# A graph layer kernel: x copied to the scratch table inside DRAM, and the SRC order's scatters moved from the node pass to the dense pass

## The reference

```python
h = x @ Wn.T + bn ; e = edge_attr @ We.T + be
a = leaky_relu(sum((h[src] + e) * attn, -1), 0.01)
a = softmax of a over the edges of one dst
z = x + relu(segment_sum(h[src] * a, dst, N))
x1 = layernorm(z)
mean = segment_sum(x1[dst], src, N) / max(count(src), 1)
out = layernorm(x1 + x1 @ W1.T + b1 + mean @ W2.T + b2)
```

## Time and profile before

| | before |
|---|---|
| median of 3 runs (lowest, highest) | 1667.97 us (1666.65, 1668.83) |
| the profiled execution's own time | 1660.1 us |
| its span | 1658.3 us |
| PE, PEld | 76%, 64% of the span |
| DVE, ACT, POOL | 66%, 47%, 45% |
| DMA, HBM read and written | 188 GB/s, 182.2 MB and 130.0 MB |
| granted TensorE clock, mean | 0.901 |

### The profile page before, as it was taken

One profiled execution on the slowest core, in us unless ns is written; L12 is line 12 of the kernel. 1 busy time (PEld: TensorE's weight loads), 2 busy tenths in 40 slices (PEclk: granted clock), 3 DMA queues, 4 the chain that ended last, 5 costly groups with the idle time before them and its releaser, 6 DMA issues.

```text
span 1658.3 us, 26818 instructions
## 1 busy us (share of the span) xinstructions
PE 1265.2 (76%) x7210; PEld 1068.7 (64%) x7210; DVE 1094.4 (66%) x3970; ACT 782.0 (47%) x1768; POOL 750.0 (45%) x731
## 2 busy tenths in 40 slices
PE   4277865776000799985099999999999899999994
PEld 3166754665000688764088888888888688877784
DVE  8565585666322655441088888888888888777762
ACT  6243475442000344332067777777777455444442
POOL 1035652035555678788642013333332256555553
PEclk9688798998555899999599999999999999999997
DMA  8977588767999555554557678888887323232221
GB/s 286 300 185 214 172 261 268 234 228 236 335 343 344 141 83 83 82 70 51 95 179 223 218 237 265 263 269 267 262 271 254 128 80 98 87 95 88 90 81 46
DMA packets 134006, 311.40 MB, mean 188 GB/s; under 512 B 24605, under 2 KB 57972, under 8 KB 133928
## 3 DMA queue, kind: packets, MB, share of 16 engines
q1 hardware_dynamic: 91870, 245.02, 44.7%
q0 software_dynamic: 40128, 64.45, 18.2%
q10 hardware_dynamic: 1930, 1.06, 0.2%
HBM read 182.23 MB, written 129.96 MB: 188 GB/s over the span
## 4 chain that ended last, share of the span: by engine, by line
PE 44%; DMA 27%; POOL 12%; issue 8%; DVE 4%; ACT 2%; SPq 2%; POOLq 0%; ACTq 0%
PE bank L1250 25%; DMA aggn<-low_digits_scratch 7%; DMA X<-in_x,idx_src 7%; PE bank L1240 6%; DMA z_scratch<-yout 5%; POOL z_scratch L513 4%; DMA xin<-z_scratch,idx_src 4%; POOL out_rows L467 4%; POOL xin L464 3%; PE bank L1247 3%; PE bank L1228 3%; DMA z_scratch<-xin,idx_out 3%; PE bank L1295 2%; PE bank L1291 2%; PE bank L1179 1%
## 5 line engine op out<-in xcount | busy, mean ns | idle before, releaser
L1250 PE MATMUL bank<-w1T,xT 128*128 128x256 f32 x1968 | 490.7, 380 | 0.0
L1250 PEld LDWEIGHTS bank<-w1T,xT 128*128 128x128 f32 x1968 | 343.3, 190 | 66.3
L473 POOL DMA_INDIRECT order_scratch<-pay,rank_i x200 | 196.8, 984 | 230.6 <-DVE rank_i L846 95.9
L568 ACT ACTIVATE yout<-bank,nmr,rstd 128x256 f32<-128x256 f32 x492 | 251.2, 576 | 8.0 <-DVE nmr L754 8.0
L919 DVE BATCH_NORM_STATS2 stats<-xin 128x6 f32<-128x512 f32 x246 | 158.7, 686 | 111.3 <-DMA xin<-z_scratch 57.6
L559 ACT COPY xT<-bank 128x512 f32<-128x512 f32 x346 | 203.0, 588 | 36.3 <-PE bank L1240 25.0
L464 POOL DMA_INDIRECT X<-z_scratch,idx_dst x100 | 94.9, 949 | 257.1 <-DVE xin L751 191.1
L919 DVE BATCH_NORM_STATS2 stats<-bank 128x6 f32<-128x512 f32 x246 | 168.5, 694 | 59.9 <-PE bank L1250 59.5
L667 ACT COPY agg<-bank 128x257 f32<-128x257 f32 (+1 forms) x200 | 74.2, 371 | 219.3 <-PE bank L1295 212.5
L513 POOL DMA_INDIRECT z_scratch<-xin,idx_out x100 | 158.2, 1582 | 40.7 <-issue 26.9
L1179 PE MATMUL bank<-X 128*128 128x196 bf16 x800 | 100.1, 261 | 99.0 <-ACT sel L654 72.8
(11 more groups left out here) (187 smaller groups left out, 1911.7 us busy)
## 6 DMA issues: line engine op xcount, KB each, us to landing
yout<-in_x SPq DMA_DIRECT2D x97, 512.0 KB, 6.1
z_scratch<-yout SPq DMA_DIRECT2D x97, 512.0 KB, 7.1
xin<-z_scratch SPq DMA_DIRECT2D x97, 512.0 KB, 5.2
out_rows<-yout SPq DMA_DIRECT2D x97, 512.0 KB, 3.4
kB<-keys_scratch SPq DMA_DIRECT2D x50, 256.0 KB, 5.1
kB<-sorted_scratch SPq DMA_DIRECT2D x50, 256.0 KB, 3.4
aggn<-low_digits_scratch SPq DMA_DIRECT2D x50, 128.0 KB, 7.1
xin<-in_edge_attr SPq DMA_DIRECT2D x12, 512.0 KB, 7.1
```

The costliest lines, as they stand in the source:

```text
L473: g.indirect_dma_start(out=order_dram[k], out_offset=bass.IndirectOffsetOnAxis(ap=rank_i[k][:, t:t + 1], axis=0), in_=pay[:, t, :], in_off ...
L568: a.activation(yout[hu][0:rows, j, :], bank_of(j // 2)[0:rows, (j % 2) * D:(j % 2 + 1) * D], ACT.Identity, bias=nmr[0:rows, slot, j:j + 1] ...
L1250: ins = mm(to, buf[:, jj, c, 0:n], w[:, c, :], start=False, stop=i == len(terms) - 1 and c == 1)
```

## The change

The copy of x no longer passes SBUF. It is cut in `NCOPY` = 100 DMAs from DRAM to DRAM. Piece c takes, from each stretch of 400 nodes, the four nodes 4c to 4c + 3: 125 rows of 4 KB, 400 KB apart, 500 KB in all. SP waits for no landing of them; POOL waits once for all before the first add. The 100 pieces stand: 8 before the fifth block of edge features, one after the loads of each of the 25 DST groups, 24 after the loads of SRC group 1 (two at a time, each pair waiting for the one-hot digits of two more groups), 11 after the loads of the odd SRC groups 3 to 23, and 32 after the SRC sort. The DST order is read at SRC group 5 and no longer 12, ScalarE's store of the sorted keys moving with it (`ORDER_AT`). `FLIGHT` is 6 and no longer 4. The two SRC order scatters after each group of the node pass are gone; 80 instead of 30 of them lie in the dense pass, two in each of its first 40 groups, and the order is read at group 48 and no longer 24 (`HOOK`), so that the 100 gathers of neighbours' rows lie between groups 56 and 92 and no longer between 32 and 92. Four instead of two of these gathers may be open.

```diff
--- before.py
+++ after.py
@@ -21,11 +21,9 @@
 BF16 = mybir.dt.bfloat16
 I32 = mybir.dt.int32
 DST, SRC = 0, 1
-ORDER_AT = 12
-FLIGHT = 4
-COPY_FIRST = 12
-COPY_ONEHOTS = 14
-HOOK = 24
+ORDER_AT = 5
+FLIGHT = 6
+HOOK = 48
 
 
 def wait(eng, sem, value):
@@ -68,6 +66,8 @@
     assert 2 * HC <= 512 and LO == 2 * P and T % 4 == 0
     EC = 2 * GT
     NEC = FT // EC
+    NCOPY = 100
+    assert N % (NCOPY * GT) == 0
 
     z_dram = nc.dram_tensor("z_scratch", [N + 6 * P, D], F32).ap()
     keyrow_dram = [nc.dram_tensor(f"keys_scratch{k}", [T, P], F32).ap() for k in (DST, SRC)]
@@ -229,8 +229,7 @@
         s_sortd = sem("sorted_keys_in_dram")
         s_xones = sem("ones_columns")
         s_xg = sems("src_rows_gathered", FLIGHT)
-        s_cin = sems("copy_loaded", 4)
-        s_cout = sems("copy_stored", 4)
+        s_copy = sem("x_copied")
         s_zero = sem("spare_rows_cleared")
 
         s_xin = sems("x_loaded", 4)
@@ -280,7 +279,7 @@
         s_enm = sem("edge_r_scales")
         s_ey = sem("edge_y_ready")
         s_xs = sems("own_z_rows_gathered", 4)
-        s_nb = sems("neighbour_z_rows_gathered", 2)
+        s_nb = sems("neighbour_z_rows_gathered", 4)
         s_zsc = sems("z_rows_added", 4)
         s_ysc = sems("y_scattered", 4)
         s_rc = sems("reciprocals", 6)
@@ -334,27 +333,22 @@
                 sp.dma_start(xin[t][:, 0:2, :], w.rearrange("(b p) k -> p b k", b=2)).then_inc(s_w, 16)
             sp.dma_start(weT, We.rearrange("(b p) k -> p b k", b=2)).then_inc(s_w, 16)
 
-            copied = [0]
-
-            def copy(n):
-
-                for c in range(copied[0], min(copied[0] + n, G + 2)):
-                    if c < G:
-                        wait(sp, s_cout[c % 4], 16 * (c // 4))
-                        sp.dma_start(full(yout[c % 4])[0:parts(c)], grp(x, c, parts(c))).then_inc(s_cin[c % 4], 16)
-                    if c >= 2:
-                        h = c - 2
-                        sp.wait_ge(s_cin[h % 4], 16 * (h // 4 + 1))
-                        sp.dma_start(grp(z_dram, h, parts(h)), full(yout[h % 4])[0:parts(h)]).then_inc(s_cout[h % 4], 16)
-                copied[0] = min(copied[0] + n, G + 2)
-
-            copy(4)
             sp.wait_ge(s_wt, 3)
             sp.wait_ge(s_vu, 1)
 
+            copied = [0]
+
+            def part_of(table):
+                return table.rearrange("(r c k) d -> c r (k d)", c=NCOPY, k=GT)
+
+            def copy_x(n):
+                for c in range(copied[0], min(copied[0] + n, NCOPY)):
+                    sp.dma_start(part_of(z_dram[0:N])[c], part_of(x)[c]).then_inc(s_copy, 16)
+                copied[0] = min(copied[0] + n, NCOPY)
+
             for c in range(NEC):
                 if c == 4:
-                    copy(COPY_FIRST)
+                    copy_x(8)
                 wait(sp, s_eau, EC * (c - 3))
                 v = edge_attr[0:NEC * EC * P].rearrange("(c t p) d -> p c t d", p=P, t=EC)
                 sp.dma_start(full(xin[c % 4]).rearrange("p (t d) -> p t d", d=DE),
@@ -376,10 +370,12 @@
                     sp.dma_start(lowB[n % 2], spread(lowrow_dram[k], q)).then_inc(s_lb[n % 2], 16)
                     wait(sp, s_kbu, n - 1)
                     sp.dma_start(full(kB[n % 2]), spread(keyrow_dram[k], q)).then_inc(s_kb[n % 2], 16)
-                    if k == SRC and q == 0:
-                        copy(COPY_ONEHOTS)
-                    elif q % 3:
-                        copy(1)
+                    if k == DST or q >= 2 and q % 2:
+                        copy_x(1)
+                    if k == SRC and q == 1:
+                        for i in range(Q // 2):
+                            sp.wait_ge(s_onehot, Q + 2 * i + 1)
+                            copy_x(2)
 
             def load3(k, q):
                 if k == DST and q < 2:
@@ -392,7 +388,7 @@
             sp.wait_ge(s_sortd, 16)
             for q in range(2):
                 load3(DST, q)
-            copy(G + 2)
+            copy_x(NCOPY)
             for q in range(2, Q):
                 load3(DST, q)
 
@@ -501,8 +497,7 @@
                 sent[0] = min(sent[0] + n, T)
 
             order_src(20)
-            for u in range(4):
-                pool.wait_ge(s_cout[u], 16 * len(range(u, G, 4)))
+            pool.wait_ge(s_copy, 16 * NCOPY)
             pool.wait_ge(s_zero, 48)
 
             for q in range(Q):
@@ -512,7 +507,6 @@
                 for j in range(GT):
                     g.indirect_dma_start(out=z_dram, out_offset=column(idx_out[DST], GT * q + j), in_=xin[q % 4][:, j, :],
                                          in_offset=None, compute_op=ALU.add).then_inc(s_zsc[q % 4], 16)
-                order_src(2)
 
             for h in range((T - sent[0]) // 2):
                 pool.wait_ge(s_x1, GT * h + GT)
@@ -523,8 +517,8 @@
             pool.wait_ge(s_agg[DST], T)
             for t in range(T):
                 pool.wait_ge(s_x1, GT * (HOOK + 8 + (G - HOOK - 14) * t // T))
-                wait(pool, s_nb[t % 2], 16 * (t // 2))
-                gather(X[:, t, 0:D], z_dram, column(idx_dst[SRC], t), s_nb[t % 2])
+                wait(pool, s_nb[t % 4], 16 * (t // 4))
+                gather(X[:, t, 0:D], z_dram, column(idx_dst[SRC], t), s_nb[t % 4])
 
             for q in range(Q + 3):
                 if q < Q:
@@ -1036,8 +1030,8 @@
                 ins.then_inc(s_nst, 1)
 
             def first_neighbours():
-                for par in range(2):
-                    dve.wait_ge(s_nb[par], 16 * len(range(par, T, 2)))
+                for i in range(4):
+                    dve.wait_ge(s_nb[i], 16 * len(range(i, T, 4)))
                 for q in range(2):
                     neighbour_stats(q, q)
```

## The result

The changed kernel takes 1707.6 us (median of 4 runs, 1705.7 to 1711.7), the kernel before 1667.6: the ratio is 1.024, 95% interval 1.022 to 1.026. It is slower by 40 us; 1715 were forecast. The profiled execution took 1711.7 us, its span 1709.9, against 1660.1 and 1658.3: in the two traces there are 51.6 us to find.

The account below looks back on a forecast made before the run. Transfers, then POOL, were taken to bound the kernel; 1660.1 profiled, +55 for the first add behind the five-engine copy's end, -8 in the node pass give 1707, +8 for the median 1715. Range 1655 to 2000 (1668 to 1765: chance 0.52).

Parts of the forecast that it names:

- price of a 4 KB row: Time of one copied row on one DMA engine: 188 ns from mixed traffic, with 154 and 308 as ends.
- fifth edge block landed: Fifth block of edge features, behind eight copy pieces: lands at 66 where before 69.5, -4 us (-10; +20).
- DST sort: 25 sort groups, each with one piece behind its loads: 5.9 us a group for 5.7, +5 us (0; +78).
- long stretch: 24 pieces after SRC group 1's loads: 113 us where before 14 blocks took 51, +62 us (+41; +134).
- rest of the SRC sort: SRC groups after the 24 pieces: one group less, -4 us; groups falling towards 4.2 to 5.0 us, -15.
- tail: sort's end to first add: Last 32 pieces after the SRC sort: 150 us, plus 15 for gathers sharing the engines and 3 to land.
- node pass: Node groups without the two scatters: 10.0 us for 10.4, -8 us in all, not the scatters' 63.
- dense and source pass: Dense pass takes 50 more scatters and denser gathers beside a busy TensorE: 0 us taken, 10 allowed.
- median against the profiled run: Median of the runs lies 8 us above the profiled execution: 1707 becomes 1715.
- "The earlier order is worth nothing under the tail": DST order read 7 groups earlier starts gathers 39 us sooner, worth nothing unless the copy ends before 534.
- a row that counts twice (308 ns): Rival on the copy: a row inside DRAM pays for read and write, 1990 us; chance 0.22.
- that second rival: Rival on the copy: 125-row pieces fill all 16 engines, first add at 450, 1546 us; chance 0.12.

Follow-up runs that it names:

- the old copy without scatters: Kernel before, copy through SBUF, with only the new order places, more gathers in flight and no scatters in the node pass: 1645.4 us, ratio 0.988.
- the pair of kernels without that wait: The 16-engine copy with two spare-row sets, POOL waiting for the group before last: 1633.2 us on chip B; the same with scatters back: 1693.7.
- the 16-engine copy: Changed kernel with 98 pieces, each one block of 512 nodes as 128 adjacent 4 KB rows: 1548.8 us, ratio 0.930 on chip A.

## Why the prediction was right, point by point

The forecast came out at 1715 for 1707.6, and by the mechanism that it named first: **five engines carry the copy, and its tail sets the first add.** The signs named for it were there: a DMA share of 0.34 in the tail, POOL's wait ended by the copy, first add at 606 for 619, a wait for `aggn` of 60 us at SRC group 2 for some 50. Ten engines in place of five took 158 us away.

But the sum was nearer than its terms, and that was luck: a price too high, a term of the wrong sign and an allowance of the wrong sign made up for each other. Each against the trace after, in shifts against before:

| step | forecast (154 ns) | measured |
|---|---|---|
| price of a 4 KB row | 188 ns (154) | 153 to 156 ns |
| fifth edge block landed | -4 (-10) | 62.0 for 69.5: -7.5 |
| DST sort | +5 (0) | 73.00 to 220.14 for 80.34 to 222.64: +4.8 |
| long stretch | +62 (+41) | 220.14 to 312.65 for 222.64 to 273.47: +41.7 |
| rest of the SRC sort | -19 (-19) | 312.65 to 466.17 for 273.47 to 406.81: +20.2 |
| tail: sort's end to first add | 168 (141) | 139.9 |
| first add | +55 (-4) | +42.1 |
| node pass | -8 | 606.0 to 868.3 for 564.0 to 822.1: +4.1 |
| dense and source pass | 0 | 843.4 for 838.0: +5.4 |
| median against the profiled run | +8 | -4.1 |

- **The price was mis-sized.** I took the mixed window's 188 ns because a copy inside DRAM reads and writes; five engines ran at the price of the best slice. With 154 ns my sum was 1656, 51 us too low.
- **The rest of the SRC sort was wrong in sign**, 39 us off, and this made up for it. I let the groups fall to 4.2 to 5.0 us because the engines' load was under 5 us. But a group waits for its load's landing, not for a mean load: behind a piece a load is 3.9 us later on five engines, and VectorE and ScalarE stood: from 331 to 466 they waited 27 and 47 us for `aggn`, with ten engines, over the same groups, 4 and 18. `aggn` took 8.6 us in the median against 7.1. The load behind the long stretch added 8 us by itself, 17.1 for 8.8, since SyncE had its queue full. The runs with ten and sixteen engines have their SRC groups at 4.6 us with the pieces in the same places.
- **The node pass gave nothing.** That the scatters lay inside the wait for the landing was right, and it is shown by the old copy without scatters, whose groups kept their distance, and by the pair of kernels without that wait. The last 0.35 us a group that I still expected were not there (10.34 for 10.4). And the keys of group 2 behind the 32 pieces, which I named without a price, cost 5 us.
- **"The earlier order is worth nothing under the tail"** was 11 us off in the changed kernel: fewer gathers share the tail.
- **The dense pass** held, with gathers from group 56 to 92: the kernel with the old copy and the new places needs 834.6 us from its first dense load to its span's end, the kernel before 836.2. Of the 5.4 us of the changed kernel's trace, 4.6 lie in the source pass, which the change does not touch; its own runs differ by 6 us. Their cause was not tried.

- **The last 8 us** took the median to lie above the profiled execution, as before; this time it lay 4 us below.

Of the rivals, a row that counts twice (308 ns) is excluded by 153 to 156 ns, all sixteen engines by the 34%. What that second rival would give, 1546, is what a copy on sixteen engines then took, 1548.8: the sum was sound there, only the condition was not met.

## What to carry to other kernels

Before a DMA is reshaped, look at the count of its outermost rows: here 125 rows of 4 KB went over 5 of the 16 engines, 100 over 10, 128 over 16, and the first alone turned a gain of 7% into a loss of 2.4%. A queue shared by bulk pieces and small loads that are waited for prices the piece twice, once in the tail and once in every load behind it. And an instruction that lies inside a wait costs nothing and its removal gives nothing: the wait (here for a landing, by way of reused spare rows) is what to take away, and that gave 2.1 us a group.

## What the hardware showed that I had not expected

- A 4 KB row copied from DRAM to DRAM costs a DMA engine 153 to 156 ns when five engines work, no more than a load (154 ns in the best slice of before). With all sixteen it is 195 ns, with the gathers beside and in packets of 16 KB.
- The Trainium skill, "DMA: Bandwidth & Descriptors", section "Latency and other measured facts", has a full rate of 214 GB/s for copies between HBM tensors, from which I had estimated 306 ns. Here the copy moved 8.59 MB in 30 us, 286 GB/s, with the gathers beside it, and with ten engines and rows 500 KB apart 8.82 MB in 35 us, 252 GB/s. The measurement decides.
- SyncE's queue takes only so much ahead, and by these runs it is not pieces that count. On five engines issuing 24 took 85 us, and a load issued then landed 17.1 us later: some four pieces of 25 rows an engine, about 110 rows. On ten engines the load behind the last piece landed 14.5 us later: some nine pieces of 10 rows an engine, about 90 rows. The 30 last pieces on sixteen engines, in packets of 16 KB, were all issued in 19.9 us, long before they were carried. The row counts are estimates from these times.
- Ten engines were as good as sixteen: beside their pieces a gather took 5.4 us to land in the median, while beside contiguous 512 KB pieces on sixteen it took 15.9 us from 350 to 380. In the kernel before, with sixteen engines as full, it took 6.4 us; what delays it, the packets of 16 KB or the many pieces queued ahead, stays open.
- The kernel before took 1666, 1731 and 1721 us on three chips. With the same program, the 16-engine copy, a DST sort group took 4.9 us on A and 6.2 us on C, with engines starting late and no releaser shown; the five-engine copy ran at the same pace there as elsewhere (132 GB/s on B, 131 where it is alone in the changed kernel). Why is not known.
